# Fills and masks before a gated-scan stack and an attention block: from GpSimd and the head of VectorE to ScalarE and the middle of VectorE

## The reference

```python
def _stack(x, Wz, bz, Wh, bh, gamma, beta):        # _mingru: z = sigmoid(Wz h + bz), t = tanh(Wh h + bh)
    h = x                                          # s = scan over time of s*clip(1 - z) + z*t
    for i in range(4):
        h_new = _mingru(h, Wz[i], bz[i], Wh[i], bh[i])
        if i > 0:
            h_new = h_new + h
        h = _layernorm(h_new, gamma, beta)
    return h
```

## Time and profile before

| What | Value |
|---|---|
| runs | 382.99, 381.34, 390.44 us |
| profiled execution | 381.31 us, span 379.6 us |
| mean granted TensorE clock | 0.897 |
| PE busy | 273.0 us, 72% |
| DVE busy | 248.7 us, 66% |
| ACT busy | 187.1 us, 49% |
| POOL busy | 151.5 us, 40% |

### The profile page before, as it was taken

One profiled execution on the slowest core, in us unless ns is written; L12 is line 12 of the kernel. 1 busy time (PEld: TensorE's weight loads), 2 busy tenths in 40 slices (PEclk: granted clock), 3 DMA queues, 4 the chain that ended last, 5 costly groups with the idle time before them and its releaser, 6 DMA issues.

```text
span 379.6 us, 8018 instructions
## 1 busy us (share of the span) xinstructions
PE 273.0 (72%) x2839; PEld 199.2 (52%) x2839; DVE 248.7 (66%) x664; ACT 187.1 (49%) x353; POOL 151.5 (40%) x337
## 2 busy tenths in 40 slices
PE   1475766776876757389889888887687887169970
PEld 0243744545554525165667667577576566147650
DVE  5997888898799641255367649758741757227772
ACT  2125489988997856054644654653431342014410
POOL 9114566667565530250015005603300524606555
PEclk9999699999998958857999999999965998869996
DMA  5899900000000300000000000100300120142000
GB/s 150 253 333 336 318 5 2 0 2 0 2 3 0 111 2 0 0 2 2 2 2 4 3 2 9 52 2 32 84 17 0 58 59 15 63 109 62 25 22 19
DMA packets 19807, 20.47 MB, mean 54 GB/s; under 512 B 1554, under 2 KB 18224, under 8 KB 19640
## 3 DMA queue, kind: packets, MB, share of 16 engines
q1 hardware_dynamic: 18392, 16.77, 15.0%
q0 software_dynamic: 1376, 3.18, 2.4%
HBM read 7.85 MB, written 12.29 MB: 53 GB/s over the span
## 4 chain that ended last, share of the span: by engine, by line
PE 28%; DVE 15%; issue 7%; ACT 4%; POOL 3%; DMA 1%; DVEq 1%; POOLq 0%; SPq 0%; ACTq 0%
PE bank L826 8%; PE scores L796 3%; DVE mneg L1379 3%; PE scores L799 2%; PE bank L612 2%; PE scores L948 2%; DVE sums L1387 2%; DVE late L1530 1%; PE scores L803 1%; DVE h_bwd L1520 1%; PE bank L742 1%; DVE h_bwd L1519 1%; PE bank L723 1%; ACT probs L1119 1%; PE bank L835 1%
## 5 line engine op out<-in xcount | busy, mean ns | idle before, releaser
L1379 DVE TENSOR_REDUCE mneg<-scores 128x8 bf16<-128x1024 f32 x32 | 39.0, 1218 | 32.1 <-PE scores L796 22.5
L1119 ACT ACTIVATE probs<-scores 128x1024 f32<-128x1024 f32 x32 | 32.8, 1024 | 54.0 <-PE scores L803 54.0
L1243 DVE TENSOR_TENSOR_SCAN early<-a_both,bank 128x512 f32<-128x512 f32 x32 | 38.8, 1211 | 6.1 <-issue 5.9
L651 PE MATMUL scores<-ident,early 128*128 128x128 f32 x64 | 19.0, 325 | 19.7 <-DVE early L1261 17.7
L434 POOL TENSOR_SCALAR a_both<-early 128x508 f32<-128x508 f32 x32 | 19.5, 610 | 29.7 <-ACT early L1022 25.7
L1387 DVE RECIPROCAL sums<-bank 128x128 f32<-128x128 f32 x16 | 15.3, 956 | 23.5 <-PE bank L826 23.4
L803 PE MATMUL scores<-mnegT,pick 32*128 32x128 bf16 x256 | 28.3, 243 | 0.0
L459 POOL TENSOR_TENSOR ln_tmp<-ln_tmp,minus_half 128x8 f32<-128x8 f32 x16 | 26.4, 1648 | 1.3
L1513 DVE TENSOR_TENSOR h_fwd<-scores,a_both 128x512 f32<-128x512 f32 x19 | 13.1, 690 | 20.5 <-PE scores L948 13.7
L612 PE MATMUL bank<-ident,early 128*128 128x128 f32 x136 | 23.4, 301 | 3.6 <-ACT h_fwd L1039 2.1
L651 PEld LDWEIGHTS scores<-ident,early 128*128 128x128 f32 x64 | 10.7, 167 | 29.2 <-issue 29.2
(11 more groups left out here) (262 smaller groups left out, 822.2 us busy)
## 6 DMA issues: line engine op xcount, KB each, us to landing
sorted_rows<-blank SPq DMA_DIRECT2D x1, 8710.0 KB, 32.6
late<-sorted_rows SPq DMA_DIRECT2D x15, 130.0 KB, 2.1
x_rows<-in_x_dram SPq DMA_DIRECT2D x4, 256.0 KB, 3.1
w_s<-in_L_ffn_W_dram SPq DMA_DIRECT2D x1, 1024.0 KB, 6.2
w_s<-in_L_ffn_W_dram SPq DMA_DIRECT2D x4, 256.0 KB, 6.9
a_both<-in_L_ffn_b_dram SPq DMA_DIRECT2D x1, 1024.0 KB, 4.8
x_rows<-sorted_rows SPq DMA_DIRECT2D x4, 130.0 KB, 2.9
ctx_rows<-in_ctx_dram SPq DMA_DIRECT2D x1, 256.0 KB, 3.3
```

The lines of the kernel that those rows point to most:

```text
L651: pe.matmul(dst, s_buf[:, k % 4, t * P:(t + 1) * P], ident[:, :], is_transpose=True, start=True, stop=False)
L1119: act.activation(probs[:, n % 2, 1 - h::2, :].rearrange("p (j i) q -> p j i q", i=2), exp_banks.rearrange("p i j q -> p j i q"), ACT.Exp, ...
L1243: dve.tensor_tensor_scan(out_s, a, b, 0.0, ALU.mult, ALU.add).then_inc(s["s_ready"], 1)
L1379: dve.tensor_reduce(mneg[:, n % 2, h::2, 0:4], max_banks, AX.X, ALU.max, negate=True).then_inc(s["mx_r"], 1)
```

## The change

GpSimd no longer fills the states, `sel` and `v_z`. ACT writes the zeros of `sel` after its first dummy activation, and the zeros of `v_z` in window 3 of layer 0, both by Identity with scale 0.0 over a broadcast view of `ident`. DVE no longer builds `pick` and `sel` between the norms of x; `masks()` is called after the layers, in front of `low_keys(0)`. In layer 0 `to_rows` no longer adds the turned state, so that the states need no zeros. The counts of pool_init are renumbered.

```diff
@@ gpsimd
             pool.memset(blank[:, :], 1.0).then_inc(s["blank_r"], 1)
-            pool.sem_inc(s["pool_init"], 1)
-            for d in range(2):
-                pool.memset(h[d][:, :], 0.0).then_inc(s["pool_init"], 1)
-
             pool.memset(minus_half[:, :], -0.5)
...
-            pool.memset(sel[:, :, :, :].bitcast(F32), 0.0).then_inc(s["pool_init"], 1)
             pool.memset(mneg[:, :, :, :], 0.0).then_inc(s["pool_init"], 1)
             pool.memset(ones_z[:, :, :], 0.0).then_inc(s["pool_init"], 1)
-            pool.memset(v_z[:, :], 0.0).then_inc(s["pool_init"], 1)
@@ tensor, to_rows
-                    pe.matmul(dst, s_buf[:, k % 4, t * P:(t + 1) * P], ident[:, :], is_transpose=True,
-                              start=True, stop=False)
+                    last = pe.matmul(dst, s_buf[:, k % 4, t * P:(t + 1) * P], ident[:, :], is_transpose=True,
+                                     start=True, stop=(n < STEPS))
+                    if n < STEPS:
+                        continue
                     last = pe.matmul(dst, src[:, t * P:(t + 1) * P], ident[:, :], is_transpose=True,
                                      start=False, stop=True)
...
-            pe.wait_ge(s["pool_init"], 3)
@@ scalar
             act.activation(key[:, :], ident[:, 0:TPC], ACT.Sigmoid)
+            zeros = ident[:, :].unsqueeze(1)
+            act.activation(sel[:, :, :, :].rearrange("p a j c -> p (a j) c"), zeros.to_broadcast([P, NHEAD, P]),
+                           ACT.Identity, scale=0.0).then_inc(s["sel_z"], 1)
             act.wait_ge(s["prep_T"], 1)
@@ scalar, end of the loop over the windows of layer 0
+                if j == 3:
+                    whole = v_z.shape[1] // P
+                    act.activation(v_z[:, 0:whole * P].rearrange("p (n c) -> p n c", c=P), zeros.to_broadcast([P, whole, P]),
+                                   ACT.Identity, scale=0.0).then_inc(s["vz_z"], 1)
+                    act.activation(v_z[:, whole * P:], ident[:, 0:v_z.shape[1] - whole * P], ACT.Identity,
+                                   scale=0.0).then_inc(s["vz_z"], 1)
@@ vector
             for chunks in ((0,), (1, 2)):
                 x_norm(chunks, x_stats(chunks))
-            dve.wait_ge(s["ident_done"], 4)
-            dve.reduce_sum(row32[:, :], ...)
...
-            last.then_inc(s["mask_done"], 1)
-            dve.wait_ge(s["pool_init"], 5)
+            dve.wait_ge(s["pool_init"], 2)
+
+            def masks():
+                ...                                 # the same six operations; waits for sel_z instead of pool_init
@@ vector, after the layers
             ch = Chain(dve, s["dve2"])
+            masks()
             low_keys(0, bank[1])
             low_queries(0, bank[0])
```

More of the change, by code:

```diff
@@ L227, in build @@
         names = """x_in0 x_in1 x_in2 x_in3 ctx_in vec_in fw_in rw_in attw_in bc_in b12_in w1_in w2_in out_done
-        ident_done pool_init mask_done x_norm x_rowsT x_cols prep_T prep_cols
+        ident_done pool_init sel_z vz_z mask_done x_norm x_rowsT x_cols prep_T prep_cols
         u_ready keep_r gated b_r decay s_ready rows_ready st_r ln_p coef n_dve n_act cols_ready h_ready dve1
@@ L478, in _ @@
             layer_norm(LAYERS - 1, PAIRS - 1)
-            pool.wait_ge(s["pool_init"], 9)
+            pool.wait_ge(s["pool_init"], 4)
             for j in range(4):
@@ L893, in _ @@
             turn_shift(0)
-            pe.wait_ge(s["pool_init"], 13)
+            pe.wait_ge(s["pool_init"], 8)
             for n in range(NT):
@@ L1105, in value_rows @@
                 if g == 0:
-                    act.wait_ge(s["pool_init"], 9)
+                    act.wait_ge(s["vz_z"], 2)
                 for j in range(4):
@@ L1212, in _ @@
                 x_norm(chunks, x_stats(chunks))
-            dve.wait_ge(s["ident_done"], 4)
[L1214 to L1222, removed]
-            last.then_inc(s["mask_done"], 1)
-            dve.wait_ge(s["pool_init"], 5)
+            dve.wait_ge(s["pool_init"], 2)
+            def masks():
+                dve.wait_ge(s["ident_done"], 4)
+                dve.reduce_sum(row32[:, :], ident[:, :].rearrange("p (i c) -> p c i", c=32),
+                               AX.X).then_inc(s["mask_done"], 1)
+                dve.wait_ge(s["mask_done"], 1)
+                dve.tensor_copy(pick[:, :, :], row32[:, 0:4].unsqueeze(2).to_broadcast([P, 4, P])).then_inc(s["mask_done"], 1)
+                dve.wait_ge(s["sel_z"], 1)
+                eye = ident[:, :].rearrange("p (h d) -> p h d", d=HD).unsqueeze(2).to_broadcast([P, NHEAD, 2, HD])
+                for i, b in enumerate((slice(0, 2), slice(2, 4), slice(0, 4, 2), slice(1, 4, 2))):
+                    blocks = sel[:, i, :, :].rearrange("p j (i b d) -> p (j i) b d", b=4, d=HD)[:, :, b, :]
+                    last = dve.tensor_scalar(blocks, eye, 1.0, None, ALU.mult)
+                last.then_inc(s["mask_done"], 1)
             def inflow(l, k, layer0=False):
@@ L1459, in _ @@
             ch = Chain(dve, s["dve2"])
+            masks()
             low_keys(0, bank[1])
             low_queries(0, bank[0])
-            dve.wait_ge(s["pool_init"], 9)
+            dve.wait_ge(s["pool_init"], 4)
             for half in range(HALVES):
```

## The result

| | before | after |
|---|---|---|
| runs of the comparison | 20 | 20 |
| median, lowest and highest | 384.69 us, 381.34 to 393.23 | 380.3 us, 376.21 to 382.43 |
| mean | 385.78 us | 379.77 us |
| profiled execution, span | 381.31 us, 379.6 | 379.72 us, 377.7 |
| mean granted clock | 0.897 | 0.869 |

What follows compares the result with a forecast made beforehand. No engine bounds the whole; DVE sets the time from 3.85 to about 34.5 us. 4.13 + 1.55 + 0.3 = 6.0 us off 381.31 gives 375.3, plus half of 1.7 is 376.2 us; 8-in-10 range 373.0 to 380.3.

Steps and rivals of the forecast that it cites:

- Part 1: Head, DVE: without GpSimd's fills of h, sel and v_z, L321 falls from 4.30 to 0.17 us, 4.13 us off.
- Part 2: Head, DVE: the masks leave, 1.55 us off; in front of low_keys DVE's idle 4.76 us covers their 1.6 us.
- Part 3: L321 at 24.18 us, slowed by GpSimd's decays: the second small stall goes, 0 to 0.33 us off, 0.3 taken.
- Parts 4 and 5: ACT writes zeros of sel (1.92 us) and v_z (2.1 us); both taken as cost 0, the latter covered by 0.04 us.
- Part 6: Layer 0, PE: 32 state transposes go; those of steps 4 and 5 pay for v_z's fill, nothing gained beyond.
- the clock in layer 0: TensorE may stay at the low clock until 40 us, about 1.5 us longer, covered by the scan's 2.31 us wait.
- the base: End of the sum: profiled 381.31 us less 6.0 gives 375.3; half the median's 1.7 us excess added, 376.2 us.
- a low stretch more 12%: Rival, 12%: TensorE's clock is lower for one or two stretches more, 1.5 to 3.0 us lost, 378.4 us.
- less 17%: Rival, 17%: one or both of the layers' low clock stretches fall away, giving 374.7 or 373.2 us.
- The price of 1.5 us for a slow turn: Dense layers: a stretch at TensorE's low clock costs 1.5 us, read from layer_norm distances of 6.32 and 7.85 us.

Runs made afterwards that it cites:

- e1: The changed kernel with the masks built at the head of VectorE again; median 379.18 us, ratio 0.9853 to the kernel before.
- e9: The kernel before with one added wait on GpSimd, a pause between two fills; median 382.45 us, ratio 0.9974.
- e2: The kernel before with only the masks moved in front of the low parts; median 385.39 us, ratio 1.0024.
- e3: The changed kernel with layer 0 adding a turned tile of zeros, so 32 transposes are back; median 379.89 us, ratio 0.9794 to the kernel before.
- e10: The changed kernel run again, unchanged; median 379.4 us, ratio 0.987 to the kernel before.
- e4: The changed kernel with memsets of unused space on VectorE, making the head as long as before; median 385.53 us, ratio 1.0043 to the kernel before.

## Why the prediction was wrong

- **Part 1** (4.13 us, L321): right. L321 takes 0.17, e1 shows 4.13 us at the first layer_norm. Its cause, GpSimd's fills and not the place of the operation, is shown by e9; that it is their overlap, as I had it, is not. The load of chunk 2 was in time.
- **Part 2** (1.55): right, 1.72 between e1 and the changed kernel, where part 3 is in it and 0.1 us of an earlier landing, and 1.59 in e2. Its cover held, 3.20 us of wait left.
- **Part 3** (0.3): the stall moved from L321 to L332 for the most part (0.33 us gone, 0.25 back); the sum of the head is 5.85 us instead of 6.0.
- **Parts 4 and 5**: the fill of sel took 1.89 us where 1.92 was the estimate, of v_z 1.92 and 0.31. The cover held and was wider than the 0.04 us I had: the scan still waits 0.49 us. The gates came 0.45 us later against the head and not 0.8, so the transposes gave 1.7 us where I had put 1.3. e3 shows that they made the cover.
- **Part 6 and the clock in layer 0**: with half of the transposes the low level did last longer in layer 0 (0.52 against 1.00 in e3; by the Trainium skill, TensorE: Matmul & The Clock Gate, Part 4, where transposes don't count as PE-busy the same way, the two would be alike; the traces speak against it), without a price, since the wait in front of the scan at 36.75 took it up (2.31 us before, 1.52 after, and 2.30 in e3).
- **The step that failed is the last one of the sum, the base.** "I add half of that" set the kernel before at 382.15 us. That was one profiled execution, with only two slow turns in the layers, and a median of three runs. Only 18 of 97 runs of before lie under 382.15 us; their median is 384.8. This is 2.5 us of the 4.1 in the comparison's medians (384.69 less 382.15).
- **The remaining 1.6 us is the gain**: 6.0 in the sum, 4.4 by the medians (6.0 by the means). The sum carried the head's gain to the end and put the low stretches behind it at nothing; in the two profiled executions they took 3.9 us of it. Whether the medians' 1.6 is more than the chance of 20 runs each isn't shown. The "1.6% less than before" is 6.0 of 382.15; against the median of 382.99 the forecast was 1.8% less.
- **The chances of the clock** were wrong in form. I gave a low stretch more 12%, less 17%, as rivals that exclude the forecast. In the traces a stretch more or less is the rule: the first trace of after has two more in the attention stage than that of before, worth 2.4 and 1.5 us, e10 neither. Nearly all of the range's width comes from them, and it had to be centred on the middle over them, 379 to 380 us. The price of 1.5 us for a slow turn was a little high: turns of 6.3 and 6.5 us alternate, and the slow ones of 7.85 stand in place of the 6.5, so 1.4. That 380.3 is still the end of the range is luck: its top was worked out from the same low base.

The profiled executions differ by 1.6 us because the lead of 5.6 us at the end of the layers met these two stretches: 5.3 - 2.4 - 1.5 and 0.2 regained. The change doesn't bring them by itself: e10 hasn't got them, and e9, without the change, has low stretches at the same steps.

## What to carry to other kernels

Look for one row out of scale before counting busy shares: a run of fills on GpSimd can hold off a small tensor_scalar operation of VectorE for all its length, and a pause between them or another engine for the fills frees it. Where a time spreads by 3% and a trace has stretches at a low clock, run the kernel before often enough first (three runs gave a median of 382.99 us, 97 gave 384.8), correct the single trace to the usual number of them before subtracting anything, and judge an edit by the lead at a fixed instruction ahead of the first such stretch. A saving on an engine with slack is not worthless if a fill is put behind it.

## What the runs showed of the hardware

- Tensor_scalar operations of VectorE waited for GpSimd's fills (L321 4.30 us, L323 1.94, ends within 0.03 us of a fill's), while the ones with two tensor inputs of the same size beside them took 0.16 us. One SBUF input alone doesn't make an operation wait: the statistics at 3.85 us, which read one, took 0.87 us under the fill of h_bwd and 0.87 without it. The Trainium skill (SBUF — State Buffer, Who interferes with whom) has an operation of VectorE with two SBUF inputs contend only with a GpSimd operation that reads SBUF, not with a fill, which only writes, and the traces agree.
- L332, with two SBUF inputs, took 0.41 us in the changed kernel under GpSimd's decays, which read SBUF (19.10 to 20.4 us). This agrees with what the same section of the Trainium skill says of two inputs against an operation that reads SBUF.
- A slow turn in the layers cost 1.4 us in nearly every case (7.85 against 6.49), once 2.7 (9.15 in e2), and a low stretch in the attention stage 1.2 to 2.4. After the same 2.1 us of TensorE work in 3.4 the clock fell in one execution and stayed in the other.
- The column PEclk reads 1.00 for the first 22 us, but there four transposes take 1.12 us (18.21) and later, at 28.46, four take 0.66. In the first stretch the duration of a row tells the level, and that column doesn't.
- A memset of 128x4096 float32 on VectorE took 3.47 us in e4 and one of 1536 elements 1.34, 0.85 and 0.87 ns per element.
- ScalarE wrote 2048 zeros per partition in 1.92 us and 120 in 0.31 (the fill of v_z), where GpSimd's fill of all 2168 took 1.91.
